# Second norm of a Mamba and mixture-of-experts block: its three VectorE steps, its GpSimd step and its TensorE steps placed earlier in the order of each slot

## The chip, the cores and the metric

The kernel runs on one core of one Trainium2 chip. The metric is the device time of one execution in microseconds; lower is better. The core has five engines that work from separate instruction queues, in order, and wait on semaphores: TensorE (PE), VectorE (DVE), ScalarE (ACT), GpSimd (POOL) and SyncE (SP), which here issues almost all transfers.

## The reference, cut to what matters

For each of 8 batches of 512 rows by 128 columns:

```
h  = layernorm(x) * (1 + ca) + sa
x1 = x + ga * mamba(h)                  # selective scan, 256 channels, 16 states
h2 = layernorm(x1) * (1 + cb) + sb      # the second norm
out = x1 + gb * moe(h2)                 # 8 experts, top 2, and one shared expert
```

In `mamba` the state of each channel follows h[t] = decay[t] * h[t-1] + input[t] over 512 steps; with 256 channels and 16 states that is 32 sequences of 128 channels. In `moe` a router gives 8 logits for each row, all experts are computed for all rows, and the two with the largest probabilities are kept by weight. All of it is fp32.

## The kernel before, in words

**Slots.** The batches go through a software pipeline that is written out by hand. In slot i, batch b = i is scanned, batch a = i - 1 goes through its output projection, its second norm and its experts, batch n = i + 1 is prepared (convolution, projections, softplus), and batch m = i + 2 gets its first norm. `pipeline` (L293) calls each engine's `slots(b, a, n, m)` for i = 0 to 7 and then a `tail` for the last batch. Slot 0 has no a, slot 6 has no m, slot 7 has no n and no m. So the second norm of batches 0 to 6 lies in slots 1 to 7, and that of batch 7 in the tail. The order of the calls in each `slots` is the order of that engine's queue.

**A unit.** The scan of a batch is cut into 16 units u of 2 x 512 elements. For each unit DVE makes the input product (L1197, `scan_input`) into two PSUM banks and then runs the scan (L1206, `scan`); ACT made the decays before (L885, `decays`); POOL multiplies the state by C (L433, `readout`); PE adds it into Y in PSUM through transposes (L516, `y_add`). There are four state buffers, so scan u waits for y_add(u - 4): scan 6 for y_add(2) and scan 7 for y_add(3). There is one input buffer, so product u waits for scan u - 1. Each readout of a slot also waits for product u + 1 (L431), which it does not read.

**The second norm of batch a in a slot.** PE's `out_proj` (L593) and `att_transpose` (L600) leave the attention output in PSUM. DVE's `residual` adds x and takes mean and variance (L1226, L1230, L1233, L1235). POOL's `make_rstd` adds epsilon and raises to -0.5 (L420, L423). DVE's `x1hat` subtracts and scales (L1244, four instructions). PE transposes it (L616, `x1_transpose`). ACT's `h2_rows` writes h2 and its rounded copy h2_hi (L992, L995). DVE's `split_h2` subtracts them (L1310). PE's `router` multiplies h2 by the router's weights (L624); DVE's `logits` (L1254, L1258, L1260) waits for that. The expert products `up` (L645 to L647, 18 groups of 3 matmuls) wait for `split_h2`, and from the fourth group on for ACT's gelu of the group three before (L1014). `keep_busy` (L611) issues transposes of the identity whose result is not used.

**ACT's order** in a slot: softplus of batch n, decays for units 6 and 7 (L885), `h2_rows`, decays for units 8 and 9, the router's exponential (L1001), a table load, 18 gelus, and then the decays of later units between the expert mixing steps. This order is the same in both kernels.

**SP** loads B and C of a group of four units in 1 MB transfers (L342); B of group 2 waits for product 3, C of group 2 for readout 3, and both are used from unit 8 on.

Of the kernel before, what the change touches and what calls it, by code (L numbers as in the profile page):

```python
# [35 lines left out]
M_UP = (E + 1) * HQ  # L36
# [24 lines left out]
def adaln_mamba_moe_kernel(nc, x, in_proj_w, conv_w, conv_b, x_proj_w, dt_w, dt_b, a_log, d_skip,  # L61
# [5 lines left out]
    with ExitStack() as ctx:  # L67
# [3 lines left out]
        def sem(name):  # L71
            return ctx.enter_context(nc.semaphore(name))
# [153 lines left out]
        stats2_done = sem("stats2_done")  # L226
        rstd2_eps = sem("rstd2_eps")
        rstd2_done = sem("rstd2_done")
        xhat2_done = sem("xhat2_done")
# [36 lines left out]
        def units_after(b, u):  # L266

            return b.i * UN + (u + 1)
# [132 lines left out]
        @block.gpsimd  # L401
        def _(pool):
            pool.memset(ident[:, :], 0.0).then_inc(const_made, 1)
            pool.memset(before[:, :, :], 1.0).then_inc(const_made, 1)
            pool.memset(minus_half, -0.5).then_inc(const_made, 1)
            pool.memset(eps_tile, EPS).then_inc(const_made, 1)
            pool.memset(dt_raw, 0.0).then_inc(const_made, 1)
            pool.memset(w9[:, :, :], 1.0).then_inc(const_made, 1)
            pool.wait_ge(const_made, 6)
            pool.affine_select(out=ident[:, :], in_=ident[:, :], pattern=[[-1, P]],  # L410
                               compare_op=ALU.not_equal, fill=1.0, base=0,
                               channel_multiplier=1).then_inc(const_made, 1)

            pool.affine_select(out=before[:, :, :], in_=before[:, :, :], pattern=[[1, E], [-1, E]],
                               compare_op=ALU.is_gt, fill=0.0, base=0,
                               channel_multiplier=0).then_inc(const_made, 1)

            def make_rstd(which, stats, eps_added, done, b):
                pool.wait_ge(stats, b.i + 1)
                pool.tensor_tensor(rstd[:, which, :], mean_var[:, which, :, 1], eps_tile,  # L420
                                   ALU.add).then_inc(eps_added, 1)
                pool.wait_ge(eps_added, b.i + 1)
                pool.tensor_tensor(rstd[:, which, :], rstd[:, which, :], minus_half,  # L423
                                   ALU.pow).then_inc(done, 1)

            def readout(b, u, paced=True):
                pair, q, first = unit(u)
                if u % (2 * Q) == 0:
                    pool.wait_ge(c_in[pair % BC_RING], b.i * 32 + 16 * (pair // BC_RING + 1))
                if paced:  # L430
                    pool.wait_ge(input_done, units_after(b, u + 1))  # L431
                pool.wait_ge(scan_done, units_after(b, u))
                pool.tensor_tensor(state[:, u % STATE_RING, :, :], state[:, u % STATE_RING, :, :],  # L433
                                   bc[:, pair % BC_RING, 1, first:first + NU, :],
                                   ALU.mult).then_inc(read_done, 1)

            def slots(b, a, n, m):
                if a:
                    readout(a, UN - 1, paced=b is not None)
                for u in range(UN - 1):  # L440
                    if b:
                        readout(b, u)
                    if a and u == 2:
                        make_rstd(1, stats2_done, rstd2_eps, rstd2_done, a)
                    if m and u == 5:
                        make_rstd(0, stats_done, rstd_eps, rstd_done, m)

            def tail(a):
                make_rstd(1, stats2_done, rstd2_eps, rstd2_done, a)

            pipeline(pool, slots, tail)

        @block.tensor
        def _(pe):
# [147 lines left out]
            def keep_busy(a, n, count):  # L604

                if n:
                    pe.wait_ge(sp_abs, Q * n.i + Q)
                else:
                    pe.wait_ge(mixmul_done, DOWNS * a.i)
                for k in range(count):  # L610
                    nc.tensor.transpose(A[1][:, 0:P], ident[:, :], ident[:, :])  # L611

            def x1_transpose(a):
                pe.wait_ge(xhat2_done, a.i + 1)
                for t in range(NT):
                    last = nc.tensor.transpose(MISC[:, t * P:(t + 1) * P], xhat2[:, t, :], ident[:, :])  # L616
                last.then_inc(x1T_done, 1)
# [82 lines left out]
            def slots(b, a, n, m):  # L700
# [37 lines left out]
                if b:  # L738
                    y_add(b, 1)
                if a:  # L740
                    keep_busy(a, n, 14)
                    x1_transpose(a)
                if b:
                    y_add(b, 2)
                if a:
                    keep_busy(a, n, 5 if b else 12)
                    router(a)
                    for k in range(M_UP):
                        up(a, n, k)
                if b:  # L750
                    y_add(b, 3)
# [342 lines left out]
        def _(dve):  # L1094
# [223 lines left out]
            def slots(b, a, n, m):  # L1318
                if b:
                    scan_input(b, 0)  # L1320
                    scan(b, 0)
                    scan_input(b, 1)
                if a:
                    gate_y(a)
                if b:
                    scan(b, 1)
                    scan_input(b, 2)
                    scan(b, 2)
                if b:
                    scan_input(b, 3)  # L1330
                if a:
                    residual(a)
                if b:
                    scan(b, 3)
                if a:
                    x1hat(a)
                if b:
                    scan_input(b, 4)
                    scan(b, 4)
                if a:  # L1340
                    split_h2(a)
                    logits(a)
                if b:
                    scan_input(b, 5)
                    scan(b, 5)
                if a:
                    top2(a)
                if b:
                    scan_input(b, 6)
                if m:  # L1350
                    stats(m)
                if b:
                    scan(b, 6)
                if m:
                    xhat(m)
                if n and n.i == 0:
                    split_up_weights()
                if b:
                    scan_input(b, 7)
                    scan(b, 7)  # L1360
                if n:
                    make_delta(n)
                for u in range(8, UN):
                    if b:
                        scan_input(b, u)
                    if a:
                        if u == UN - 1:
                            finish(a)
                    if b:
                        scan(b, u)  # L1370
                    if n and u == 12:
                        delta_x(n)
# [84 lines left out]
```

## Time and profile before

| | us |
|---|---|
| three runs | 684.22, 689.11, 687.82 |
| median | 687.82 |
| the profiled execution's own time | 684.8 |
| its span, first to last instruction | 683.1 |
| DVE busy | 598.3 (88%) |
| PE busy | 593.3 (87%) |
| ACT busy | 489.7 (72%) |
| POOL busy | 320.2 (47%) |

A row of the timeline reads: start in microseconds from the span's start, duration, engine, line, operation, output from inputs, shapes, count of instructions merged in the row, and in brackets the engine's idle time ahead of it with what ended it. Durations of instructions that follow each other on an engine overlap slightly, so distances between starts are used for sums. The mean granted TensorE clock is 0.955 of full speed.

### The profile page before, as it was taken

The numbers are of one execution on the slowest core, as the hardware profiler recorded it, in microseconds if no ns is written. First come the engines' busy times: TensorE is split into PE (matmuls) and PEld (weight loads), VectorE is DVE, ScalarE is ACT, GpSimd is POOL, SyncE is SP. The second block draws the span as 40 slices with busy tenths as digits, with TensorE's granted clock in tenths as the row PEclk, the third lists the DMA queues.
The fourth block names the chain that finished last, engine by engine and source line by source line (L and its number), as shares of the span: only waits on it lengthen the run. The fifth ranks groups of instructions, "written<-read, shape, count | busy, mean of one in ns | idle before, by whom it ended". The sixth has DMA issues, their size and how long they took to land.

```text
span 683.1 us, 9767 instructions
## 1 busy us (share of the span) xinstructions
PE 593.3 (87%) x3646; PEld 466.5 (68%) x3646; DVE 598.3 (88%) x713; ACT 489.7 (72%) x861; POOL 320.2 (47%) x171
## 2 busy tenths in 40 slices
PE   5684478899989998999989998999979947998897
PEld 4243345689657965788567966787668936798686
DVE  5399999999999999999999999999998999798416
ACT  3689535999589976989589957998598925962460
POOL 1036556446654556446653656446543664464000
PEclk9787589999999999999999999999999968999999
DMA  7423333314432235133531343223522442220000
GB/s 221 161 92 140 123 139 142 125 70 169 163 128 82 108 128 184 62 124 124 173 124 63 124 160 138 83 103 124 179 103 70 176 156 83 103 78 16 1 1 16
DMA packets 26705, 77.87 MB, mean 114 GB/s; under 512 B 3025, under 2 KB 17570, under 8 KB 18466
## 3 DMA queue, kind: packets, MB, share of 16 engines
q1 hardware_dynamic: 26178, 76.82, 31.1%
q8 instruction: 29, 0.48, 0.3%
q10 hardware_dynamic: 480, 0.43, 0.2%
q14 instruction: 18, 0.15, 0.1%
HBM read 74.61 MB, written 2.62 MB: 113 GB/s over the span
## 4 chain that ended last, share of the span: by engine, by line
PE 53%; DVE 31%; issue 7%; ACT 5%; POOL 2%; DMA 1%; DVEq 0%; POOLq 0%; ACTq 0%
DVE state L1206 15%; PE psum L677 12%; PE psum L516 10%; DVE psum L1197 8%; PE psum L543 5%; PE psum L645 5%; PE psum L647 4%; PE psum L646 4%; PE psum L687 3%; POOL state L433 2%; PE psum L662 2%; PE psum L565 1%; ACT L866 1%; DVE out_sb L1244 1%; PE psum L799 1%
## 5 line engine op out<-in xcount | busy, mean ns | idle before, releaser
L433 POOL TENSOR_TENSOR state<-state,bc 128x1024 f32<-128x1024 f32 x127 | 300.1, 2363 | 291.8 <-DVE psum L1197 291.8
L1206 DVE TENSOR_TENSOR_SCAN state<-decay,psum 128x1024 f32<-128x1024 f32 x128 | 292.2, 2283 | 21.9 <-PE psum L516 9.5
L885 ACT ACTIVATE decay<-delta,a_neg 128x511 f32<-128x511 f32 x256 | 166.1, 729 | 10.4 <-DVE state L1206 10.3
L516 PE MATMUL psum<-ident,state 128*128 128x128 f32 x1024 | 139.0, 283 | 33.6 <-POOL state L433 33.4
L1197 DVE TENSOR_TENSOR psum<-bc,du 128x1024 f32<-128x1024 f32 x128 | 157.6, 1231 | 4.8 <-DVE state L1206 0.5
L516 PEld LDWEIGHTS psum<-ident,state 128*128 128x128 f32 x1024 | 120.3, 146 | 56.0 <-POOL state L433 44.9
L677 PE MATMUL psum<-down_w,h 128*128 128x128 f32 x896 | 109.9, 276 | 0.0
L677 PEld LDWEIGHTS psum<-down_w,h 128*128 128x128 f32 x896 | 104.4, 192 | 5.3 <-issue 5.3
L1014 ACT ACTIVATE h<-psum,vec 128x512 f32<-128x512 f32 x144 | 97.0, 688 | 2.1 <-PE psum L647 0.6
L980 ACT ACTIVATE gT_mix<-psum,w 128x128 f32<-128x128 f32 x224 | 64.8, 388 | 20.0 <-PE psum L687 14.4
L645 PE MATMUL psum<-h_hi,up_hi 128*128 128x512 f32 x144 | 59.2, 411 | 10.7 <-DVE h_lo L1310 6.7
L543 PE MATMUL psum<-h_sb,conv_in_wT 128*128 128x512 f32 x128 | 59.9, 614 | 8.8 <-ACT h_sb L895 8.8
L647 PE MATMUL psum<-h_hi,up_lo 128*128 128x512 f32 x144 | 57.7, 401 | 0.0
L646 PE MATMUL psum<-h_lo,up_hi 128*128 128x512 f32 x144 | 57.6, 400 | 0.0
L543 PEld LDWEIGHTS psum<-h_sb,conv_in_wT 128*128 128x128 f32 x128 | 24.3, 199 | 34.6 <-issue 25.4
L645 PEld LDWEIGHTS psum<-h_hi,up_hi 128*128 128x128 f32 x144 | 27.5, 191 | 20.5 <-DVE h_lo L1310 7.3
L687 PE MATMUL psum<-ident,gT_mix 128*128 128x128 f32 x224 | 33.9, 274 | 0.0
L647 PEld LDWEIGHTS psum<-h_hi,up_lo 128*128 128x128 f32 x144 | 27.4, 190 | 6.7
L646 PEld LDWEIGHTS psum<-h_lo,up_hi 128*128 128x128 f32 x144 | 27.6, 191 | 6.0
L687 PEld LDWEIGHTS psum<-ident,gT_mix 128*128 128x128 f32 x224 | 26.0, 141 | 1.5 <-ACT gT_mix L980 1.5
L611 PE MATMUL psum<-ident 128*128 128x128 f32 x210 | 26.2, 273 | 0.0
L906 ACT ACTIVATE du<-psum,vec 128x512 f32<-128x512 f32 x16 | 10.8, 687 | 21.2 <-PE psum L543 18.7
(151 smaller groups left out, 638.3 us busy)
## 6 DMA issues: line engine op xcount, KB each, us to landing
bc<-bc_rows SPq DMA_DIRECT2D x64, 1024.0 KB, 4.7
x_sb<-_attn_hidden_states_dram SPq DMA_DIRECT2D x9, 256.0 KB, 2.8
x<-_attn_hidden_states_dram SPq DMA_DIRECT2D x7, 256.0 KB, 3.0
out_dram<-out_sb SPq DMA_DIRECT2D x7, 256.0 KB, 2.4
h<-in_L_ffn_rw_dram SPq DMA_DIRECT2D x1, 1024.0 KB
bc_rows<-rows SPq DMA_DIRECT2D x8, 64.0 KB, 4.8
h<-in_L_wmod_dram ACTq DMA_DIRECT2D x1, 384.0 KB
h<-in_L_attn_in_proj_w_dram SPq DMA_DIRECT2D x1, 256.0 KB, 4.7
```

The source lines that it names most:

```text
L433: pool.tensor_tensor(state[:, u % STATE_RING, :, :], state[:, u % STATE_RING, :, :], bc[:, pair % BC_RING, 1, first:first + NU, :], ALU.mu ...
L516: last = nc.tensor.matmul(Y[q][:, t * P:(t + 1) * P], state[:, u % STATE_RING, s, t * P:(t + 1) * P], ident[:, :], start=False, stop=(u in ...
L543: last = nc.tensor.matmul(A[q], conv_in_wT[:, q, k, :], h_sb[:, k:k + L], start=(k == 0), stop=(k == KC - 1))
L645: nc.tensor.matmul(bank, high, h2_hi[:, :], start=True, stop=False)
L646: nc.tensor.matmul(bank, high, h2_lo[:, :], start=False, stop=False)
L647: nc.tensor.matmul(bank, low, h2_hi[:, :], start=False, stop=True).then_inc(up_done, 1)
L677: last = nc.tensor.matmul(A[j % 2][:, e * DM:(e + 1) * DM], h1[:, (group * EG + e) * HQ + q, ts], down_w[:, group * EG + e, q, :], start=( ...
L687: last = nc.tensor.matmul(OUTP[:, t * P:(t + 1) * P], mix[:, j % 2, e, :], ident[:, :], start=False, stop=(j == DOWNS - 1 and e == EG - 1) ...
L885: last = nc.scalar.activation(decay[:, r, s, 1:L], delta[:, b.p, q, 1:L], ACT.Exp, scale=a_neg[:, q, k:k + 1])
L1014: nc.scalar.activation(h1[:, m, :], UP_RING[m % 3], ACT.Gelu, bias=vec[:, bias:bias + 1]).then_inc(gelu_done, 1)
L1197: nc.vector.tensor_tensor(IN, bc[:, pair % BC_RING, 0, first:first + NU, :], du[:, b.p, q:q + 1, :].broadcast_to([P, NU, L]), ALU.mult).th ...
L1206: nc.vector.tensor_tensor_scan(state[:, u % STATE_RING, :, :].rearrange("p n t -> p (n t)"), decay[:, u % DECAY_RING, :, :].rearrange("p n ...
```

## The change

Nothing is computed differently. On DVE, `residual` moves from behind product 3 to ahead of it, `x1hat` from behind scan 3 to ahead of it, and `split_h2` with `logits` from behind scan 4 to ahead of product 4. On POOL, `make_rstd(1)` moves from behind readout 2 to ahead of it, and POOL then waits for `x1hat` before it begins readout 2. On PE, `x1_transpose` comes after 8 instead of 14 idle transposes, `router` after 10 instead of 5 more, and `y_add(2)` moves from behind `x1_transpose` to behind the third `up` group. In the slot without b the counts would be 14 and 12, but no slot with a lacks b. ACT, SP and all tails stay as they are.

```diff
 # POOL, slots
                 for u in range(UN - 1):
+                    if a and u == 2:
+                        make_rstd(1, stats2_done, rstd2_eps, rstd2_done, a)
+                        pool.wait_ge(xhat2_done, a.i + 1)
                     if b:
                         readout(b, u)
-                    if a and u == 2:
-                        make_rstd(1, stats2_done, rstd2_eps, rstd2_done, a)
 # PE, slots
                 if a:
-                    keep_busy(a, n, 14)
+                    keep_busy(a, n, 8)
                     x1_transpose(a)
+                    keep_busy(a, n, 10)
+                    router(a)
+                    for k in range(3):
+                        up(a, n, k)
                 if b:
                     y_add(b, 2)
                 if a:
-                    keep_busy(a, n, 5 if b else 12)
-                    router(a)
-                    for k in range(M_UP):
+                    for k in range(3, M_UP):
                         up(a, n, k)
 # DVE, slots
                     scan(b, 2)
+                if a:
+                    residual(a)
                 if b:
                     scan_input(b, 3)
                 if a:
-                    residual(a)
+                    x1hat(a)
                 if b:
                     scan(b, 3)
                 if a:
-                    x1hat(a)
+                    split_h2(a)
+                    logits(a)
                 if b:
                     scan_input(b, 4)
                     scan(b, 4)
-                if a:
-                    split_h2(a)
-                    logits(a)
-                if b:
                     scan_input(b, 5)
                     scan(b, 5)
```

## Rows read from the trace of the kernel before

**Rows 1.** The page: the span, and each engine's busy time with its instructions.

```profile
span 683.1 us, 9767 instructions
...
PE 593.3 (87%) x3646; PEld 466.5 (68%) x3646; DVE 598.3 (88%) x713; ACT 489.7 (72%) x861; POOL 320.2 (47%) x171
```

**Rows 2.** Windows: bounds, length, busy of PE, PEld, DVE, ACT, POOL, clock, DMA.

```profile
268.40:343.25 74.85, 70.44 (x447) 55.32 (x445) 71.06 (x81) 61.41 (x111) 40.00 (x20) 1.00 0.34 125
...
555.00:565.00 10.00, 6.50 (x30) 5.70 (x30) 8.87 (x7) 0.82 (x1) 4.68 (x2) 0.50 0.63 231
```

**Rows 3.** Waits of the whole span: waiter, releaser, total us, times, longest.

```profile
DVE state L1206 <- PE psum L516: 9.5, 7, 4.0
```

**Rows 4.** Timeline of DVE in slot 3, from the residual to scan 7.

```profile
268.05 0.69 DVE L1226 TENSOR_TENSOR x<-psum,x 128x512 f32<-128x512 f32 x1
...
269.98 2.25 DVE L1206 TENSOR_TENSOR_SCAN state<-decay,psum 128x1024 f32<-128x1024 f32 x1
272.15 1.09 DVE L1244 TENSOR_SCALAR out_sb<-x,mean_var,rstd 128x128 f32<-128x128 f32 x4
273.15 1.23 DVE L1197 TENSOR_TENSOR psum<-bc,du 128x1024 f32<-128x1024 f32 x1
274.51 2.29 DVE L1206 TENSOR_TENSOR_SCAN state<-decay,psum 128x1024 f32<-128x1024 f32 x1
...
277.30 0.18 DVE L1254 TENSOR_TENSOR gT_mix<-psum,router_bias 128x32 f32<-128x32 f32 x1
...
277.85 1.23 DVE L1197 TENSOR_TENSOR psum<-bc,du 128x1024 f32<-128x1024 f32 x1
...
290.36 1.23 DVE L1197 TENSOR_TENSOR psum<-bc,du 128x1024 f32<-128x1024 f32 x1
292.11 2.29 DVE L1206 TENSOR_TENSOR_SCAN state<-decay,psum 128x1024 f32<-128x1024 f32 x1 [0.53 <-PE psum L516]
```

**Rows 5.** Timeline of POOL in slot 3: readout 2.

```profile
268.22 2.38 POOL L433 TENSOR_TENSOR state<-state,bc 128x1024 f32<-128x1024 f32 x1 [1.34 <-DVE psum L1197]
```

**Rows 6.** Timeline of PE in slot 3: att_transpose, x1_transpose, router.

```profile
266.41 0.65 PE L600 MATMUL psum<-ident,h 128*128 128x128 f32 x4
...
273.30 0.66 PE L616 MATMUL psum<-ident,out_sb 128*128 128x128 f32 x4 [1.75 <-DVE out_sb L1244]
...
275.49 1.06 PE L624 MATMUL psum<-router_sb,h 128*128 128x8 f32 x8
```

**Rows 7.** Timeline of ACT in slot 3: decays 6 and 7, then h2_rows.

```profile
270.43 2.54 ACT L885 ACTIVATE decay<-delta,a_neg 128x511 f32<-128x511 f32 x4
273.99 0.78 ACT L992 ACTIVATE h<-psum,modT 128x512 f32<-128x512 f32 x1 [1.02 <-PE psum L616]
```

**Rows 8.** Timeline of the tail, where each step waits for the one before.

```profile
635.88 0.66 PE L600 MATMUL psum<-ident,h 128*128 128x128 f32 x4 [0.23 <-ACT h L969]
...
636.65 0.69 DVE L1226 TENSOR_TENSOR x_sb<-psum,x_sb 128x512 f32<-128x512 f32 x1 [5.79 <-PE psum L600]
...
638.75 0.20 POOL L420 TENSOR_TENSOR rstd<-mean_var,constants 128x4 f32<-128x4 f32 x1 [12.10 <-DVE mean_var L1235]
...
640.07 1.11 DVE L1244 TENSOR_SCALAR out_sb<-x_sb,mean_var,rstd 128x128 f32<-128x128 f32 x4 [1.40 <-POOL rstd L423]
...
643.42 1.06 PE L624 MATMUL psum<-router_sb,h 128*128 128x8 f32 x8 [0.45 <-ACT h_hi L995]
644.52 0.19 DVE L1254 TENSOR_TENSOR gT_mix<-psum,router_bias 128x32 f32<-128x32 f32 x1 [3.34 <-PE psum L624]
```

**Rows 9.** Timeline of DVE in slot 6: scan 7.

```profile
517.52 2.29 DVE L1206 TENSOR_TENSOR_SCAN state<-decay,psum 128x1024 f32<-128x1024 f32 x1 [2.85 <-PE psum L516]
```

**Rows 10.** Timeline of slot 7: the residual on DVE and h2_rows on ACT.

```profile
569.50 0.69 DVE L1226 TENSOR_TENSOR x<-psum,x 128x512 f32<-128x512 f32 x1 [0.23 <-PE psum L600]
...
575.44 0.78 ACT L992 ACTIVATE h<-psum,modT 128x512 f32<-128x512 f32 x1 [4.32 <-PE psum L616]
```

**Rows 11.** The page's DMA issues: count, KB each, us from issue to landing.

```profile
bc<-bc_rows SPq DMA_DIRECT2D x64, 1024.0 KB, 4.7
```

More of the change, by code:

```diff
@@ L1331, in slots @@
                 if a:
-                    residual(a)
+                    x1hat(a)
                 if b:
                     scan(b, 3)
-                if a:
-                    x1hat(a)
-                if b:
-                    scan_input(b, 4)
-                    scan(b, 4)
                 if a:
@@ L1343, in slots @@
                 if b:
+                    scan_input(b, 4)
+                    scan(b, 4)
                     scan_input(b, 5)
```

## The prediction

> **What bounds the kernel now.** I began with the page's head: DVE is busy for 598.3 of 683.1 us and PE for 593.3, so neither share alone decides [rows 1]. The windows by slot do: in slot 3 DVE's instructions fill 71.06 of 74.85 us, at full TensorE clock, and most of the rest is the few hundredths between instructions that follow each other [rows 2]. I then read the waits of DVE. In the slots it has only one repeated wait that this change can touch: scan 7 waits for `y_add(3)`, seven times, 9.5 us in all [rows 3]. Five of them are the 0.53 us of slot 3; slot 6 has 2.85 us and slot 7 the longest, 4.0 us, since there DVE has no first norm of a later batch to do meanwhile [rows 4, 9]. So in slots 1 to 5 DVE sets the pace and every microsecond that it stands still is paid, while in slots 6 and 7 the chain through ACT and PE to `y_add(3)` sets it. That is the question to put to each step: does DVE still find its operand ready?
>
> **Today's cover.** Between `residual` and `x1hat` DVE has scan 3; between `x1hat` and `split_h2` it has product 4 and scan 4 [rows 4]. Thus POOL's two steps, the transpose, ACT's two copies and the router run beside scans. The change takes scans out of both gaps. I work it through in slot 3 and write R for the new start of `residual`.
>
> **Residual.** In the tail, where nothing hides the chain, `residual` begins 0.77 us after `att_transpose` (635.88 to 636.65) [rows 8]. In slot 3 that transpose starts at 266.41 [rows 6], so R = 267.18. PE reaches it through `gate_y`, ACT's copy and `out_proj`, all untouched. The operation is today at 268.05, behind product 3; DVE will be free some 0.3 us before R and waits. The next DVE instruction can start 1.93 us after it (268.05 to 269.98) [rows 4]: product 3 at R + 1.93, ending 1.23 later at R + 3.16.
>
> **POOL's steps and x1hat.** In the tail the epsilon step starts 2.10 us after `residual`, and `x1hat` 1.32 us after that [rows 8], so at best `x1hat` is at R + 3.42. Now POOL would work beside product 3, and no row has that. One end of the price is zero: readout 2 ran beside today's `residual` in its usual 2.38 us [rows 5], and POOL's power step ran beside a scan. The other end is that POOL stands until the product ends: epsilon step at about R + 3.23, `x1hat` at R + 4.55, 1.13 us more. A gain is excluded, the two POOL instructions being the same. By nearness the rows with a scan or the residual speak for zero, but these read one operand from PSUM, whereas the product reads both from SBUF, as POOL's own steps do. That difference is in the very resource that two engines could share, so I take the late end, without much certainty, and keep the other as a rival.
>
> The Trainium skill (SBUF — State Buffer, Who interferes with whom) says that a DVE instruction with two SBUF inputs contends with a GpSimd instruction that reads SBUF, and that the one that started first holds the port for its whole length. By it the sum would be the late end; the rows only agree in that nothing with a PSUM operand was slowed, and no run here shows the conflict itself.
>
> **Transpose, h2_rows, router.** `x1_transpose` follows `x1hat` by 1.15 us (272.15 to 273.30) and `h2_rows` the transpose by 0.69 (273.99) [rows 4, 6, 7]. ACT is free at 272.97, when decays 6 and 7 end [rows 7]; ACT's order did not change. So `h2_rows` starts at R + 6.39 = 273.57, only 0.42 us sooner than today. With POOL undisturbed it would be ready at R + 5.26 = 272.44 and would wait for ACT until 273.0. The router follows `h2_rows` by 1.50 (273.99 to 275.49) [rows 6, 7]: 275.07. `logits` can start 1.10 after the router (643.42 to 644.52) [rows 8]: 276.17. `split_h2` fits in between. DVE ended scan 3 long before: `x1hat` at 271.73, scan 3 from about 272.73, done at about 275.0, so it waits for h2_hi briefly and then for the router.
>
> **Units 4 and 5.** Product 4 follows the start of `logits` by 0.55 (277.30 to 277.85) [rows 4]: 276.72. Scan 4 starts 1.36 later and product 5 another 2.3 after that [rows 4], 280.4. Today product 5 is at 277.85, with the same DVE work behind it. **DVE is 2.55 us later.** Up to product 7 nothing changes. Scan 7 was ready at 290.36 + 1.36 = 291.72 and started at 292.11, for PE's sake; its own readiness becomes 294.27 [rows 4]. PE delivers `y_add(3)` a little earlier than before, so that old wait is gone: 0.39 us back. Net 2.16 us a slot, and behind scan 7 DVE has no wait that could absorb it. Slots 1 to 5: 5 x 2.16 = 10.8 us.
>
> **Slot 6.** Scan 7 was ready 2.71 us before its start at 517.52 (the shown 2.85 less the 0.14 that a product and its scan always keep), so 514.81 [rows 9]. With 2.55 added it is 517.36; PE's delivery moves 0.42 earlier, to 517.10. DVE decides: -0.16.
>
> **Slot 7.** `residual` already waits, 569.50 [rows 10]. `h2_rows` comes at 569.50 + 6.39 = 575.89 against 575.44, so the `up` groups and `y_add(3)` come 0.45 later; scan 7, which waited 4.0 us [rows 3], still waits. +0.45.
>
> **What costs nothing.** `y_add(2)` behind three `up` groups: it lands in the time in which the fourth group waits for the first gelu, and scan 6 comes only after units 4 and 5 and the ranking. If that cover failed, scan 6 would wait for it. One idle transpose fewer in all. Readout 2 is held until `x1hat` is done, near R + 5.7 instead of 268.22, and ends near 275.3; behind it on POOL stand readout 3 and the rest, which wait for product 4 (276.72) anyway. If POOL and `split_h2` shared something, the split would start at 275.3 instead of 275.1, still inside the router's time. PE's first `up` needs the split, about 276.0, against 277.44 today, and the fourth waits for gelu 0, which follows `h2_rows`. SP's load of B for group 2 is issued at the end of product 3, 270.3, and C's behind readout 3, at about 280.5; each takes 4.7 us [rows 11] and both are in place by 285.2, while scan 7 is not over before 294. The store of batch a - 1 that `x1hat` waits for was issued several scans earlier. The tail and slot 0 are not touched.
>
> **Sum.** 10.8 - 0.16 + 0.45 = +11.1 us. Against the profiled execution's 684.8 that gives 695.9; that execution is 3.0 us under the median 687.82, against which it gives 698.9. I put the forecast between, at 697.
>
> **Rivals.** *POOL is not held up beside product 3.* Then `h2_rows` is bound by ACT at 273.0, router 274.5, logits 275.6, product 4 at 276.15, product 5 at 279.8: 1.97 us later than today, 1.58 net at scan 7, 7.9 in five slots. Slot 6: 514.81 + 1.97 = 516.78 against PE's 517.52 - 0.99 = 516.53, so -0.74; slot 7: `h2_rows` at 569.50 + 5.26 = 574.76, -0.68. Sum +6.5: 691.3 by the profile, 694.3 by the median. For it: no row shows a slowed POOL. 0.24.
>
> *PE, not DVE, sets the pace in ordinary executions, and the change is faster.* The place is scan 7. The profiled execution is the quick one of its kind; if in the others PE brings `y_add(3)` later than DVE could use it by more than 2.5 us instead of 0.39, DVE's new waits are free and what counts is that `h2_rows` starts up to 0.99 us sooner: 7 x 0.99 = 6.9 us less, 680.9 by the median. Against it: slots 1 to 5 all show the same half microsecond. 0.08.
>
> *Nothing to speak of happens*, because the new waits on DVE overlap with waits I did not see behind scan 7, and only a net of 0 to 3 us is left: 685 to 691. Against it: the windows leave DVE less than 4 us of 74.85 [rows 2]. 0.10.
>
> *The clock falls.* PE idles 1.75 us ahead of `x1_transpose` today [rows 6] and would idle about 2.1, plus shorter gaps, with eight idle transposes instead of 14. The slots run at 1.00; from 555 to 565 us, when PE had little to do, it was granted 0.50, the lower level of 1.2 GHz [rows 2]. If half clock lasted 8 us from there in each slot, PE would lose 4 us; it has 2.6 in hand at scan 7, so 1.4 more in each of five slots: 704. 0.06.
>
> The forecast itself has 0.52.
>
> **Range and chances.** The rival with a free POOL on the low basis gives 691.3 and the change without effect on the median 688; the upper end is the forecast on the median, 698.9, with 0.5 us more in each of five slots. Leaving out the fast rival and the fallen clock, 689 to 702. Differences below 1% (6.9 us) can hardly be told from no change. Slower by over 1%: nearly all of the forecast, a third of the free POOL, whose 6.5 us lie at the border, and the clock, 0.64. Faster by over 1%: most of the second rival, 0.06. The rest, 0.30.
>
> **What would show it.** Right: DVE waits ahead of `residual` (0.3 us), `x1hat` (about 1.4 us, on POOL's power step), `split_h2` and `logits` (together some 0.7 us); POOL's epsilon step beginning only at the end of product 3; no wait left at scan 7 in slots 1 to 5; slots 1 to 5 each some 2.2 us longer. `x1hat` at R + 3.4 would be the first rival. Wrong altogether: a slot length unchanged, or scan 7 still waiting for PE.

## The result, and the profile after

| | before | changed |
|---|---|---|
| median of the first comparison | 686.02 | 697.14 |
| ratio, 95% interval | | 1.0149 (1.0100 to 1.0198) |
| repeated in five rounds: medians | 687.53 | 697.11 |
| ratio, 95% interval | | 1.0113 (1.0078 to 1.0149) |
| profiled execution, span | 683.1 | 695.5 |
| mean granted clock | 0.955 | 0.945 |

The change makes the kernel slower, by 1.5% in the first comparison and 1.1% in the second; 697 had been forecast. Over all comparisons the kernel before was timed 23 times, at 683.3 to 692.1 us; its five executions of 691.5 us and more had mean grants of 0.938 to 0.941, so the profile, at 0.955, is of one of the quick ones. Line numbers on DVE are 3 higher and on PE 1 higher than before. The page's head of the changed kernel:

```profile
span 695.5 us, 9753 instructions
...
PE 604.8 (87%) x3639; PEld 473.1 (68%) x3639; DVE 600.9 (86%) x713; ACT 491.3 (71%) x861; POOL 326.8 (47%) x171
```

DVE's work grew by 2.6 us, the span by 12.4 [rows 1]: DVE is not doing more, it stands still. DVE's waits in slot 3 of the changed kernel (waiter, releaser, total, times, longest):

```profile
DVE out_sb L1247 <- POOL rstd L423: 1.2, 1, 1.2
DVE psum L1200 <- DVE state L1209: 0.5, 1, 0.5
DVE x_sb L1161 <- POOL rstd L423: 0.4, 1, 0.4
DVE gT_mix L1257 <- PE psum L625: 0.4, 1, 0.4
DVE x L1229 <- PE psum L601: 0.3, 1, 0.3
```

Scan 7's wait for PE is gone, and three new ones are there: the residual for the attention transpose, `x1hat` for POOL, `logits` for the router. The same in DVE's timeline of slot 3, to be laid beside [rows 4]:

```profile
272.99 0.69 DVE L1229 TENSOR_TENSOR x<-psum,x 128x512 f32<-128x512 f32 x1 [0.30 <-PE psum L601]
...
274.92 1.21 DVE L1200 TENSOR_TENSOR psum<-bc,du 128x1024 f32<-128x1024 f32 x1
277.29 1.12 DVE L1247 TENSOR_SCALAR out_sb<-x,mean_var,rstd 128x128 f32<-128x128 f32 x4 [1.17 <-POOL rstd L423]
278.32 2.28 DVE L1209 TENSOR_TENSOR_SCAN state<-decay,psum 128x1024 f32<-128x1024 f32 x1
280.64 0.75 DVE L1313 TENSOR_TENSOR h_lo<-h,h_hi 128x512 fp32r<-128x512 f32 x1
281.76 0.19 DVE L1257 TENSOR_TENSOR gT_mix<-psum,router_bias 128x32 f32<-128x32 f32 x1 [0.36 <-PE psum L625]
...
282.31 1.23 DVE L1200 TENSOR_TENSOR psum<-bc,du 128x1024 f32<-128x1024 f32 x1
...
285.99 1.23 DVE L1200 TENSOR_TENSOR psum<-bc,du 128x1024 f32<-128x1024 f32 x1
...
299.87 2.29 DVE L1209 TENSOR_TENSOR_SCAN state<-decay,psum 128x1024 f32<-128x1024 f32 x1
```

And POOL beside it:

```profile
275.08 1.09 POOL L420 TENSOR_TENSOR rstd<-mean_var,constants 128x4 f32<-128x4 f32 x1 [2.39 <-DVE mean_var L1238]
276.25 1.01 POOL L423 TENSOR_TENSOR rstd<-rstd,constants 128x4 f32<-128x4 f32 x1
278.49 2.36 POOL L433 TENSOR_TENSOR state<-state,bc 128x1024 f32<-128x1024 f32 x1 [1.23 <-DVE out_sb L1247]
```

POOL's epsilon step on four elements per partition takes 1.09 us instead of 0.20 [rows 8]. It starts 0.16 us behind product 3 and ends at 276.17, product 3 at 276.13. The rest of the chain, PE and ACT, answers to [rows 6, 7]:

```profile
272.22 0.65 PE L601 MATMUL psum<-ident,h 128*128 128x128 f32 x4
...
278.46 0.66 PE L617 MATMUL psum<-ident,out_sb 128*128 128x128 f32 x4
...
280.66 1.06 PE L625 MATMUL psum<-router_sb,h 128*128 128x8 f32 x8 [0.45 <-ACT h_hi L998]
```

```profile
276.23 2.54 ACT L888 ACTIVATE decay<-delta,a_neg 128x511 f32<-128x511 f32 x4
279.16 0.78 ACT L995 ACTIVATE h<-psum,modT 128x512 f32<-128x512 f32 x1 [0.39 <-PE psum L617]
```

**Where the 12.4 us lie.** I took the start of each slot's first scan from both timelines:

| stretch | before | changed | difference |
|---|---|---|---|
| up to slot 1's first scan (106.24, 108.42) | 106.24 | 108.42 | +2.18 |
| slot 1 | 74.85 | 76.89 | +2.04 |
| slot 2 | 75.03 | 76.79 | +1.76 |
| slot 3 | 75.37 | 77.14 | +1.77 |
| slot 4 | 74.83 | 76.80 | +1.97 |
| slot 5 | 75.02 | 76.79 | +1.77 |
| slot 6 | 75.20 | 74.44 | -0.76 |
| slot 7, first to last scan | 68.31 | 68.41 | +0.10 |
| last scan to the end | 58.25 | 59.82 | +1.57 |

Slots 1 to 5 give 9.3 us and slots 1 to 7 together 8.7. The rest, 3.7 us, lies where the code is the same. The start is scatter between executions: in the profile of the repeat (the run after_again below) slot 1's first scan is at 105.57. In the tail the clock differs. Windows over the first groups of `up` there, before and changed (length, busy of PE, PEld, DVE, ACT, POOL, clock, DMA):

```profile
645.00:650.00 5.00, 4.18 (x18) 3.41 (x19) 3.45 (x11) 4.74 (x8) 0.00 (x0) 1.00 0.00 0
```

```profile
655.80:660.80 5.00, 4.08 (x11) 3.26 (x12) 3.52 (x12) 3.23 (x6) 0.00 (x0) 0.66 0.00 0
```

In both kernels PE had idled just before for want of `split_h2` (1.33 us in the kernel before). Only in the second did the grant fall, and 11 matmuls were issued instead of 18. Why it fell there is not shown. From the last scan to the end the profiles of all the other kernels below take 59.8 to 59.9 us as well (unpaced 60.6), pe_alone and late_slots among them, which do not have DVE's and POOL's new order in slots 1 to 5; the 58.25 us were seen once.

The grant fell in the slots too, ahead of `x1_transpose` in slots 1, 3 and 5. Slot 3:

```profile
275.00:277.00 2.00, 2.00 (x12) 2.00 (x11) 1.12 (x2) 1.97 (x4) 1.84 (x2) 0.50 0.00 0
```

There it cost nothing: slots 3 and 5, where it fell, grew by as much as slot 2, where it did not, and in the profile of the repeat it did not fall in slots 1 to 5 at all, while each is as long to within 0.1 us.

Slot 7 is another matter. In the kernel before the grant was 0.57 from 580 to 584 us, in its first `up` groups; in the changed kernel's first profile it stayed full there, and in the repeat it was half for 10 us:

```profile
583.00:593.00 10.00, 9.43 (x35) 8.46 (x36) 7.80 (x10) 7.35 (x12) 4.73 (x2) 0.50 0.22 88
```

So the +0.10 us of slot 7 compare two different clocks.

### The profile page after: what moved, and what is told of

Same layout as the page of the kernel before. It is cut to its first block, busy times and chain, and to the rows that moved or that the text cites. A ratio compares the mean times of both kernels' runs of the same rounds, so it can differ in the third digit from the quotient of the medians.

```text
span 695.5 us, 9753 instructions
## 1 busy us (share of the span) xinstructions
PE 604.8 (87%) x3639; PEld 473.1 (68%) x3639; DVE 600.9 (86%) x713; ACT 491.3 (71%) x861; POOL 326.8 (47%) x171
## 4 chain that ended last, share of the span: by engine, by line
DVE 47%; PE 28%; ACT 9%; issue 8%; POOL 5%; DMA 1%; DVEq 1%; POOLq 0%; ACTq 0%
DVE state L1209 22%; DVE psum L1200 14%; PE psum L646 3%; PE psum L647 3%; PE psum L648 3%; POOL state L433 3%; PE psum L544 3%; PE psum L517 2%; PE psum L594 2%; PE psum L556 2%; ACT decay L888 1%; PE psum L573 1%; DVE delta L1179 1%; DVE delta L1173 1%; DVE du L1189 1%
## 5 line engine op out<-in xcount | busy, mean ns | idle before, releaser
L517 PE MATMUL psum<-ident,state 128*128 128x128 f32 x1024 | 144.7, 291 | 42.2 <-POOL state L433 41.9
L517 PEld LDWEIGHTS psum<-ident,state 128*128 128x128 f32 x1024 | 124.0, 150 | 69.2 <-POOL state L433 55.6
L544 PE MATMUL psum<-h_sb,conv_in_wT 128*128 128x512 f32 x128 | 63.0, 640 | 9.2 <-ACT h_sb L898 9.2
L420 POOL TENSOR_TENSOR rstd<-mean_var,constants 128x4 f32<-128x4 f32 x16 | 9.4, 590 | 44.2 <-DVE mean_var L1238 30.5
```

The source lines that it names most:

```text
L517: last = nc.tensor.matmul(Y[q][:, t * P:(t + 1) * P], state[:, u % STATE_RING, s, t * P:(t + 1) * P], ident[:, :], start=False, stop=(u in ...
L544: last = nc.tensor.matmul(A[q], conv_in_wT[:, q, k, :], h_sb[:, k:k + L], start=(k == 0), stop=(k == KC - 1))
```

## The experiments

Theory A, from the forecast: DVE loses because no scan stands any longer between the links of the chain residual, POOL, `x1hat`, PE, ACT, router, `logits`. Theory B: the loss is the conflict between POOL and DVE alone, or PE's new order. These two hold for the list as a whole; each expectation says what its own A and B are, and the verdicts below are on those. All ratios are to the kernel before, measured beside it.

**after_again.** No edit.

> The changed kernel unaltered, timed in five rounds beside the kernel before. Its first profile was 12.4 us longer than that of before, but 2.2 us of that lie ahead of slot 0's scan 7 and 1.5 us in the tail, where the code is the same. Theory A: those 3.7 us are scatter between executions; only the slots pay, by their rows 1.77 to 2.04 us in each of slots 1 to 5, -0.8 in slot 6, +0.1 in slot 7, 8.7 us in all, and the ratio is about 1.013. Theory B: the tail and the start are longer because of the change; then the profile again shows the start some 2 us and the tail some 1.5 us longer than before, and the ratio is about 1.018.

Measured: ratio 1.0113 (1.0078 to 1.0149). The slots repeat to 0.1 us (76.89, 76.76, 77.11, 76.75, 76.77, 74.43), the start is 2.85 us shorter, slot 7 is 2.9 us longer, from its first to its last scan 71.35. The tail has its 1.5 us again. So the start is scatter and slot 7 varies by some 3 us with identical code. The tail's 1.5 us came in both profiles of this kernel, but also in those of pe_alone and late_slots; since there is only one profile of the kernel before, it stays open what its other executions do there. Theory A holds for the slots and the start; of theory B only the tail came back.

**product_first.** Product 3 back ahead of the residual.

```diff
                     scan(b, 2)
+                    scan_input(b, 3)
                 if a:
                     residual(a)
-                if b:
-                    scan_input(b, 3)
                 if a:
                     x1hat(a)
```

> The changed kernel with product 3 put back ahead of residual (DVE: scan 2, product 3, residual, x1hat, scan 3, split_h2, logits, product 4). POOL's two steps then run beside nothing of DVE. Theory A (what costs is that no scan stands between the links of the chain): residual starts 0.87 us later than in the changed kernel and DVE stands still for 1.5 us ahead of x1hat, the epsilon step is back to 0.2 us, product 5 of slot 3 comes 2.29 us later than in the kernel before, and the sum by the rows is 5 x 1.90 - 0.6 - 0.7 = +8.2 us against before: the same as the changed kernel within 1 us. Theory B (what costs is the epsilon step held up beside product 3, 0.88 us a slot): 7 x 0.88 = 6 us come back, +2.5 us against before.

Measured: 694.46 against 687.53, ratio 1.0087 (1.0054 to 1.0120). DVE and POOL in slot 3 of it:

```profile
270.95 0.68 DVE L1229 TENSOR_TENSOR x<-psum,x 128x512 f32<-128x512 f32 x1
...
274.35 1.12 DVE L1247 TENSOR_SCALAR out_sb<-x,mean_var,rstd 128x128 f32<-128x128 f32 x4 [1.40 <-POOL rstd L423]
```

```profile
273.03 0.20 POOL L420 TENSOR_TENSOR rstd<-mean_var,constants 128x4 f32<-128x4 f32 x1 [3.26 <-DVE mean_var L1238]
```

The conflict is gone (0.20 us) and `x1hat` follows the residual by 3.40 us. The slots are 76.85, 76.74, 77.10, 76.74, 76.72, 74.39: within 0.07 us of the changed kernel's. Theory A: theory B had 0.88 us a slot come back. The median is 2.65 us below the changed kernel's 697.11; between the two profiles (692.7 and 695.4 us) 2.6 us of that lie in slot 7 (68.75 and 71.35), which was 68.41 in the changed kernel's first profile. Whether product_first is a little quicker than the changed kernel is therefore not shown. The epsilon step's delay of 0.89 us is what the changed order pays for starting the residual 0.87 us earlier; either order leaves the chain as long, measured from the slot's start.

**pe_pool_alone.** The parts on PE and POOL without the part on DVE. Against the changed kernel:

```diff
                     scan(b, 2)
+                if b:
+                    scan_input(b, 3)
                 if a:
                     residual(a)
                 if b:
-                    scan_input(b, 3)
+                    scan(b, 3)
                 if a:
                     x1hat(a)
                 if b:
-                    scan(b, 3)
+                    scan_input(b, 4)
+                    scan(b, 4)
                 if a:
                     split_h2(a)
                     logits(a)
                 if b:
-                    scan_input(b, 4)
-                    scan(b, 4)
                     scan_input(b, 5)
```

> Only the PE and POOL parts of the change; DVE's order is that of before. Theory A (all the cost is in DVE's order): the chain to h2_rows, router and split_h2 is timed by DVE as before, readout 2 is held until x1hat at 273.2 and ends near 275.7 (slot 3), which only readout 3 could feel by 1.2 us, and y_add(2) fits into the wait for the first gelu: within 1 us of before, ratio 1.000. Theory B (holding readout 2, or y_add(2) behind the third up group, costs): scan 6 or scan 7 waits for PE longer than the 0.53 us of before, +0.5 us or more in each of seven slots, ratio 1.005 or more.

Measured: 711.56, ratio 1.0339 (1.0299 to 1.0380). Theory B: holding readout 2 costs, and far more than the 0.5 us a slot named as the least. POOL and DVE in slot 3 of it:

```profile
279.63 5.57 POOL L433 TENSOR_TENSOR state<-state,bc 128x1024 f32<-128x1024 f32 x2 [1.89 <-DVE out_sb L1247]
```

```profile
279.47 1.22 DVE L1200 TENSOR_TENSOR psum<-bc,du 128x1024 f32<-128x1024 f32 x1
...
283.03 2.73 DVE L1313 TENSOR_TENSOR h_lo<-h,h_hi 128x512 fp32r<-128x512 f32 x1
...
301.96 2.29 DVE L1209 TENSOR_TENSOR_SCAN state<-decay,psum 128x1024 f32<-128x1024 f32 x1 [2.00 <-PE psum L517]
```

```profile
286.00:288.00 2.00, 2.00 (x5) 1.62 (x6) 1.83 (x4) 1.63 (x4) 0.41 (x1) 0.50 0.93 385
```

POOL holds readout 2 until `x1hat` is done, and with DVE's old order that is the moment when product 4 begins. Two readouts take 5.57 us instead of 4.7, and the second is still running when `split_h2` is due: 2.73 us instead of 0.67. The `up` groups start that much later, PE stands still until they can, and behind that gap its grant is 0.50. Scan 7 comes 3.53 us later behind the slot's first scan than in the kernel before (39.52 and 35.99): 2.06 us are `split_h2`, and the remaining 1.5 us fit the half clock. POOL's wait did no harm where a scan follows `x1hat` (changed kernel, product_first) and did where a product follows it.

**pe_alone.** The part on PE alone: the run above without POOL's part.

```diff
-                    if a and u == 2:
-                        make_rstd(1, stats2_done, rstd2_eps, rstd2_done, a)
-                        pool.wait_ge(xhat2_done, a.i + 1)
                     if b:
                         readout(b, u)
+                    if a and u == 2:
+                        make_rstd(1, stats2_done, rstd2_eps, rstd2_done, a)
```

> Only the PE part of the change (fewer idle transposes ahead of x1_transpose, more behind, y_add(2) behind the third up group); POOL and DVE as before. With POOL's part as well the kernel was 24 us slower, and split_h2 took 2.73 instead of 0.67 us while POOL ran readout 3. Theory A (all of that comes from POOL's wait for x1hat, which pushes readouts 2 and 3 on and readout 3 into split_h2): without it split_h2 is back at 0.67 us and the kernel is within 1.5 us of before. Theory B (PE's order costs, for instance y_add(2) late for scan 6, or the clock falls for want of idle transposes): 5 to 24 us slower than before, with scan 6 or scan 7 waiting for PE by more than 0.53 us.

Measured: 688.99 against 686.24, ratio 1.0044 (1.0008 to 1.0081); slots of 75.11, 75.11, 75.45, 74.91, 75.12, 75.30 us. `split_h2` is back at 0.67 us. Theory A in kind: `y_add(2)` behind three `up` groups and the other counts of idle transposes cost at most 0.3 us in each of slots 1 to 6, and 1.3 us in slots 1 to 7 together; the median is 2.75 us up, more than the 1.5 us that theory A allowed. Some 21 of pe_pool_alone's 24 us came from POOL's part.

**dve_alone.** The part on DVE with PE and POOL as before.

Against the kernel before:

```diff
                     scan(b, 2)
+                if a:
+                    residual(a)
                 if b:
                     scan_input(b, 3)
                 if a:
-                    residual(a)
+                    x1hat(a)
                 if b:
                     scan(b, 3)
                 if a:
-                    x1hat(a)
+                    split_h2(a)
+                    logits(a)
                 if b:
                     scan_input(b, 4)
                     scan(b, 4)
-                if a:
-                    split_h2(a)
-                    logits(a)
-                if b:
                     scan_input(b, 5)
                     scan(b, 5)
```

> Only the DVE part of the change; PE and POOL keep the order of before, so POOL runs readout 2 ahead of the epsilon step. Theory A (DVE waits for the whole chain, link by link): readout 2 starts when product 3 ends, R + 3.2, and ends at R + 5.55; x1hat comes at R + 6.95 instead of R + 4.30; product 5 of slot 3 comes 4.95 us later than before, net 4.56 at scan 7; slots 1 to 5 give 22.8 us, slot 6 +2.0, slot 7 +2.9: +27.7 us, ratio 1.040. Theory B (the loss sits elsewhere, in PE's order or in the wait for x1hat on POOL): no slower than the changed kernel, ratio 1.015 or less.

Measured: 722.28, ratio 1.0492 (1.0455 to 1.0529), 7 us above theory A. POOL and DVE in slot 3 of it:

```profile
280.05 2.36 POOL L433 TENSOR_TENSOR state<-state,bc 128x1024 f32<-128x1024 f32 x1 [3.51 <-DVE psum L1197]
282.37 0.20 POOL L420 TENSOR_TENSOR rstd<-mean_var,constants 128x4 f32<-128x4 f32 x1
```

```profile
276.83 0.69 DVE L1226 TENSOR_TENSOR x<-psum,x 128x512 f32<-128x512 f32 x1 [0.30 <-PE psum L600]
...
283.69 1.11 DVE L1244 TENSOR_SCALAR out_sb<-x,mean_var,rstd 128x128 f32<-128x128 f32 x4 [3.72 <-POOL rstd L423]
...
290.29 0.19 DVE L1254 TENSOR_TENSOR gT_mix<-psum,router_bias 128x32 f32<-128x32 f32 x1 [2.10 <-PE psum L624]
```

`x1hat` comes at R + 6.86, where 6.95 was expected. What the expectation left out is the clock: PE, idle for longer, is granted half of it through the router and the first `up` groups:

```profile
284.00:288.00 4.00, 3.14 (x15) 3.14 (x16) 3.50 (x6) 1.99 (x4) 0.00 (x0) 0.50 0.00 0
```

That the clock makes the surplus is seen within this run: in slot 1 PE idled just as long (3.66 us ahead of `x1_transpose`) but the grant stayed full, and the slot is 79.44 us, 4.59 longer than before where 4.56 were expected; in slots 2 to 5 the grant fell and they are 80.77 to 81.82 us, 5.7 to 6.6 longer. PE's old order has a share in it, since `y_add(2)` and five idle transposes stand at half clock between transpose and router.

So DVE's part needs POOL's part (`x1hat` at R + 6.86 instead of R + 4.30), and POOL's part needs DVE's. DVE's and POOL's parts together without PE's were not run.

**no_hold.** The changed kernel without POOL's wait.

```diff
                         make_rstd(1, stats2_done, rstd2_eps, rstd2_done, a)
-                        pool.wait_ge(xhat2_done, a.i + 1)
```

> The changed kernel without POOL's wait for x1hat ahead of readout 2. Readout 2 may then start right after the power step, at R + 4.3, just when x1hat becomes ready. Theory A (x1hat, a subtract and multiply from SBUF to SBUF, or what follows it, is held up by a readout that started first): x1hat's four instructions take up to 2.4 us longer in all, x1_transpose and all behind it with them, up to 2.3 us a slot and 15 us in all, ratio 1.035. Theory B (no conflict between these two): x1hat stays at 1.12 us, readout 2 merely ends 1.2 us sooner, and the time is that of the changed kernel, ratio about 1.013.

Measured: 715.53, ratio 1.0415 (1.0369 to 1.0461). Theory A; slot 3, POOL and DVE:

```profile
280.19 2.35 POOL L433 TENSOR_TENSOR state<-state,bc 128x1024 f32<-128x1024 f32 x1
```

```profile
280.26 3.13 DVE L1246 TENSOR_SCALAR out_sb<-x,mean_var,rstd 128x128 f32<-128x128 f32 x4 [1.17 <-POOL rstd L423]
```

The readout began 0.07 us ahead of `x1hat`, and `x1hat` took 3.13 us instead of 1.12. Behind it the grant is again low: 0.52 from 282 to 287 us and 0.50 from 287 to 292. Slots 1 to 6 are 2.9 to 3.5 us longer than the changed kernel's; `x1hat` accounts for 2.0 of that, and the rest, 0.9 to 1.5, is put down to the clock.

**unpaced.** The kernel before, its readouts no longer held to the products.

```diff
-                    readout(a, UN - 1, paced=b is not None)
+                    readout(a, UN - 1, paced=False)
...
-                        readout(b, u)
+                        readout(b, u, paced=False)
```

> The kernel before, with the readouts no longer waiting for product u + 1: readout u may start as soon as scan u is done, which is when product u + 1 starts on DVE. It has 120 places where a POOL instruction of 2.36 us meets a DVE product of 1.23 us with both operands in SBUF. Theory A (the two cannot run together, the one that started first keeps the other out): either the readout's record grows from 2.36 to about 3.5 us, ending where it ended before, and the total changes by less than 1%, or, where the readout starts first, the product's record grows by up to 2.3 us and the kernel is slower by tens of us. Theory B (no conflict): readouts of 2.36 us that start 1.3 us earlier, products of 1.23 us, total unchanged.

Measured: 799.68, ratio 1.1627 (1.1567 to 1.1687). DVE and POOL at two places of it, and the two groups over all of it:

```profile
270.99 1.23 DVE L1197 TENSOR_TENSOR psum<-bc,du 128x1024 f32<-128x1024 f32 x1
...
274.74 3.42 DVE L1197 TENSOR_TENSOR psum<-bc,du 128x1024 f32<-128x1024 f32 x1
```

```profile
271.03 3.41 POOL L433 TENSOR_TENSOR state<-state,bc 128x1024 f32<-128x1024 f32 x1 [0.29 <-DVE state L1206]
274.72 2.36 POOL L433 TENSOR_TENSOR state<-state,bc 128x1024 f32<-128x1024 f32 x1 [0.28 <-DVE state L1206]
```

```profile
L433 POOL TENSOR_TENSOR state<-state,bc 128x1024 f32<-128x1024 f32 x127 | 384.3, 3026 | 292.4 <-DVE state L1206 292.4
...
L1197 DVE TENSOR_TENSOR psum<-bc,du 128x1024 f32<-128x1024 f32 x128 | 209.2, 1634 | 4.8 <-DVE state L1206 0.5
```

At 271 the product starts 0.04 us ahead and the readout is held for 1.05 us; at 274.7 the readout starts 0.02 us ahead and the product is held for 2.2. Neither is slowed in part: the later one waits out the earlier, to within 0.15 us of the end of its record. The Trainium skill (SBUF — State Buffer, Who interferes with whom) says that a DVE instruction with two SBUF inputs contends with a GpSimd instruction that reads SBUF, and that the port they share is an exclusive lock; both rows agree.

Such holds are nearly the whole price. DVE's busy time grew from 598.3 to 712.6 us, by 114.3, and the span by 112.5. The products have 51.6 us of it (209.2 instead of 157.6). Most of the rest is in other DVE steps that now meet a readout: `x1hat` 14.3 us, the same step of the first norm (L1158) 12.2, a one-operand step on 128x1024 (L1173) 2.48 us instead of 0.69 each time, and two steps on only 128x32 (L1260, L1272) 1.23 and 1.94 us on average instead of 0.19.

**late_slots.** An attempt to beat both: the kernel before in slots 1 to 5, the order of product_first with the change's PE and POOL parts in slots 6 and 7, and in slot 7 decays 8 and 9 behind the gelus. DVE's part and ACT's, against the kernel before:

```diff
+                late = b and b.i >= B - 2
                 if a:
                     residual(a)
+                if late and a:
+                    x1hat(a)
                 if b:
                     scan(b, 3)
-                if a:
+                if a and not late:
                     x1hat(a)
+                if late and a:
+                    split_h2(a)
+                    logits(a)
...
-                if b:
+                last = b and b.i == B - 1
+                if b and not last:
                     decays(b, AHEAD + 2)
...
+                if last:
+                    decays(b, AHEAD + 2)
+                    decays(b, AHEAD + 3)
```

> An attempt at a faster version. The kernel before in slots 1 to 5, where DVE sets the pace. In slots 6 and 7, where the chain to y_add(3) does, the second norm early without the conflict (DVE: product 3, residual, x1hat, scan 3, split_h2, logits, product 4; POOL and PE as in the change); and in slot 7 ACT's decays 8 and 9 behind the gelus. From the rows: slot 6 as in the run with product 3 first, 74.4 instead of 75.2 us; in slot 7 logits come 1.4 us earlier, and scan 7 with them, to about 593.3 instead of 594.7, unless the clock falls there as it did in two other runs (then nothing is gained). Together 2.2 us less than before, ratio 0.997, which these rounds can hardly tell from 1; the profile can. Rival: decays 8 and 9 come too late behind the gelus and a table load, and scan 8 of slot 7 waits for them, ratio 1.000 or above.

Measured: 684.69 against 686.24, ratio 0.9976 (0.9945 to 1.0008): not told apart from 1. In the profile slot 6 is 74.59 instead of 75.20 us, and scan 7 of slot 7 stands 37.42 us behind the slot's first scan instead of 38.16:

```profile
597.67 2.29 DVE L1217 TENSOR_TENSOR_SCAN state<-decay,psum 128x1024 f32<-128x1024 f32 x1 [0.48 <-PE psum L520]
```

Its wait is down from 4.0 us [rows 3] to 0.48: DVE itself arrives later, so the two slots give 1.35 us where 2.2 were expected. Slot 6 is also short in the changed kernel and in product_first (74.44, 74.39). In slot 7 the order is not the only difference: the grant stayed full through its `up` groups, where it was 0.57 for 4 us in the kernel before.

The profiled execution as a whole is 4.4 us longer than that of the kernel before (687.5 and 683.1): 2.0 at the start, 1.6 in the tail, and 2.3 in slots 1 to 3, less 1.5 in slots 6 and 7. In slots 1 to 3 the order is that of before, yet they are 75.72, 75.74 and 76.11 us instead of 74.85, 75.03 and 75.37. Slot 3, scan 7 and a window over the first `up` groups:

```profile
296.41 2.29 DVE L1217 TENSOR_TENSOR_SCAN state<-decay,psum 128x1024 f32<-128x1024 f32 x1 [1.27 <-PE psum L520]
```

```profile
282.00:284.00 2.00, 2.00 (x6) 1.58 (x5) 1.87 (x2) 1.87 (x4) 1.22 (x1) 0.50 1.01 414
```

Scan 7 waits 1.42, 1.27 and 1.27 us for `y_add(3)` there, not 0.53. So the order of before has executions in which PE's clock sets the pace of some slots.

## Why the prediction was right

**DVE sets the pace in slots 1 to 5, PE in slots 6 and 7.** Shown for slots 1 to 6. The same steps were moved in all seven; slots 1 to 5 grew, slot 6 shrank, and in slots 1 to 6 scan 7 has no wait for PE left. For slot 7 it is open. I wrote that scan 7 would still wait there for PE; in the changed kernel product 7 comes 3.75 us later behind the first scan (36.67 and 32.92), which uses up nearly all of the old 4.0 us: 0.48 are left, 1.51 in the repeat. `h2_rows` is 0.77 us later, not 0.45 (19.67 and 18.90 behind the first scan).

**The residual's wait.** 0.30 us, as forecast. R itself lies 0.17 us earlier than worked out: `att_transpose` comes 10.12 us behind the slot's first scan instead of 10.29, as PE is ahead of DVE by then.

**POOL beside product 3.** The end I took was right in kind and 0.25 us too long: `x1hat` is at R + 4.30, not R + 4.55. I had the epsilon step begin when the product ends; its record begins at once and ends with the product, so only the power step and the semaphore come behind. What the prediction could only choose, this row and unpaced show directly, and the rival with a free POOL falls.

**Down to product 5.** From `x1hat`, the transpose follows by 1.17 us (1.15), `h2_rows` by 0.70 (0.69), the router by 1.50 (1.50), `logits` by 1.10 (1.10), product 4 by 0.55 (0.55). Steps taken from rows in which each waits for the one before, most from slot 3 and the last of the chain to `logits` from the tail, carried over to within 0.02 us. Of the 0.7 us of waits ahead of `split_h2` and `logits` only 0.36 came, all ahead of `logits`: scan 3 and `h2_rows` ended together, so `split_h2` did not wait. Product 5 of slot 3 is 23.89 us behind the slot's first scan, before 21.73 (277.85 - 256.12): 2.16 us later instead of 2.55. The two sizes above, 0.25 and 0.17, are that difference to within 0.03.

**Net per slot.** Less 0.39 for scan 7's old wait that makes 1.77 us, which is what slots 2, 3 and 5 show; 2.16 had been forecast. Slots 1 and 4 show 2.04 and 1.97: in the kernel before DVE already reached its second scan sooner there (4.62 us behind the first in slot 4, 4.79 in slot 5), so the 0.17 us could not be won again. Five slots give 9.3 instead of 10.8 us, slot 6 -0.76 instead of -0.16, slot 7 +0.10 instead of +0.45: 8.7 against 11.1. The mis-sized term is DVE's lateness of 2.55 us at product 5; with 2.16 in its place slot 6 would come to -0.55, and its last 0.2 us stay open, as does slot 7 for the clock's sake. The median came out at the forecast because 697 stands between two bases and the executions scatter by more than the 2.4 us between the sums; 3.7 of the profile's 12.4 us, moreover, lie where the code is the same. That closeness is luck.

**What I had at nothing.** `y_add(2)` and the counts of idle transposes: at most 0.3 us in each of slots 1 to 6, by pe_alone. POOL's wait for `x1hat`: right in this order, since scan 3 follows and covers readout 2; some 21 us in all if the cover fails, by the difference of pe_pool_alone and pe_alone, part of it the clock's. I named readout 2 running into `split_h2`, but not what readout 3 would do to it in another order. In the changed kernel readout 2 just touches it: `split_h2` takes 0.75 instead of 0.67 us, hidden by the router.

**The rival in which PE sets the pace.** It needed executions of the kernel before in which PE is more than 2.5 us later than DVE could use it. The longest wait seen at scan 7 in slots 1 to 5 under the old order is 1.42 us, in late_slots. The rival falls on size; that such executions exist at all, the prediction had only from the scatter of the totals.

**The clock.** The rival with a fallen clock had the grant fall behind PE's wait for `x1hat`, in every slot. In the changed kernel's first profile it fell ahead of `x1_transpose` in slots 1, 3 and 5, for 3 to 4 us, each time while PE was at work and without a gap of PE ahead of the transpose, and the lengths show that it cost nothing; in the repeat it did not fall there at all. In dve_alone and no_hold it did fall where the rival has it, and their slots are 0.9 to 2.1 us longer than the rest of the account gives, where the rival had 1.4. So its price was about right and its case did not come. What brings the fall is not shown: the same gap of 3.66 us had none behind it in slot 1 of dve_alone and one in slot 3.

## What to carry to other kernels

On an engine that is busy all the time, a step placed earlier gains nothing and pays for every link whose answer is not there yet; the useful question is what independent work stands between two links, and whether it is as long as the link. Where steps are moved on two engines that wait for each other, the parts belong together: POOL's part without DVE's and DVE's without POOL's each cost two to four times what the whole change did. And where two engines keep each other out, it is the order of starts that sets the price, so look at what a moved wait lets run side by side.

## What the runs showed of the hardware

A GpSimd instruction that reads SBUF and a VectorE instruction with both operands in SBUF exclude each other at every size seen here: POOL's step on four elements waits 0.89 us for a product, `split_h2` waits 2.06 us for a readout (2.73 against 0.67), and in unpaced DVE's two steps on 128x32 take 1.23 and 1.94 us on average instead of 0.19. The one that starts later waits for the other; a start 0.02 us ahead is enough (unpaced). VectorE instructions with one operand in PSUM ran beside readouts undisturbed [rows 5], and so did the mean and variance steps of the residual, with a single operand from SBUF (0.87 us for the four of L1230, with or without a readout beside them). The subtract and multiply of `x1hat` has a single tensor operand as well, but is held up, by 2.0 us in no_hold. In the records such a wait is no idle time: it is counted in the duration of the instruction held up, so a duration above the usual one is the sign to look for.

A chain through several engines that leaves TensorE idle can cost more than its length: in dve_alone and no_hold the grant fell to 0.50, the lower level of 1.2 GHz, behind such a gap, and their medians are 7 and 5 us above what was expected without it. It does not do so each time (slot 1 of dve_alone), and it fell without a longer gap too (late_slots, slots 1 to 3).
